# An attention and FFN block on 8 cores: two steps of post work per slot in the first four heads, and two more empty steps after the first LayerNorm

## What is computed

```python
q, k, v = split(x @ Wq + bq), split(x @ Wk + bk), split(x @ Wv + bv)
pattern = einsum('bhid,bhjd->bhij', k, q) * scale      # keys i, queries j
prob = softmax(pattern, axis=-2)                       # over the keys
out = einsum('bhis,bhid->bhsd', prob, v)
x = layernorm(x + concat(out) @ Wo + bo)
h = gelu(x @ w1 + b1)                                  # 1024 -> 4096
x = layernorm(x + h @ w2 + b2)                         # 4096 -> 1024
# x: (8, 4096, 1024) float32
```

## Time and profile before

| | us |
|---|---|
| three runs, median (lowest, highest) | 4659.8 (4652.1, 4875.7) |
| the profiled execution | 4654.3 |
| its span, slowest core (all cores 4628.1 to 4652.4) | 4652.4 |
| TensorE busy | 3593.5 (77%) |
| ScalarE busy | 2305.2 (50%) |
| VectorE busy | 1492.0 (32%) |
| one exp (L812), mean, 2048 of them | 1.023 |

### The profile page before, as it was taken

One profiled execution on the slowest core, in us unless ns is written; L12 is line 12 of the kernel. 1 busy time (PEld: TensorE's weight loads), 2 busy tenths in 40 slices (PEclk: granted clock), 3 DMA queues, 4 the chain that ended last, 5 costly groups with the idle time before them and its releaser, 6 DMA issues.

```text
span 4652.4 us, 57786 instructions; the slowest of 8 cores (4628.1 to 4652.4 us)
## 1 busy us (share of the span) xinstructions
PE 3593.5 (77%) x19264; PEld 1205.1 (26%) x19264; DVE 1492.0 (32%) x1942; ACT 2305.2 (50%) x2191; POOL 193.7 (4%) x344
## 2 busy tenths in 40 slices
PE   4365697887897798778877888788878887888766
PEld 2122242222232232222222222222222222222222
DVE  1133341114223422342234323332333232424243
ACT  0000004884557555765566556655665556555610
POOL 0011100000000000000000000000000000000000
PEclk9677798998999899999998999999999999999977
DMA  8866512113432233133412341234222322332143
GB/s 169 178 158 145 146 64 96 55 55 93 107 78 78 84 94 100 69 93 82 111 60 84 93 113 65 84 88 107 76 84 80 91 82 92 88 84 82 57 89 77
DMA packets 746247, 433.76 MB, mean 93 GB/s; under 512 B 679269, under 2 KB 695781, under 8 KB 728553
## 3 DMA queue, kind: packets, MB, share of 16 engines
q1 hardware_dynamic: 706714, 237.12, 20.7%
q0 software_dynamic: 39248, 192.96, 14.0%
HBM read 377.59 MB, written 77.59 MB: 98 GB/s over the span
## 4 chain that ended last, share of the span: by engine, by line
PE 57%; ACT 14%; DVE 11%; DMA 10%; issue 6%; POOL 1%; SPq 1%; DVEq 0%; ACTq 0%; POOLq 0%
ACT es_sb L812 11%; PE ps_o L822 11%; PE ps_s L799 9%; PE ps_d L834 6%; PE ps_w L668 5%; PE ps_g L712 5%; PE ps_w L712 5%; PE ps_g L668 4%; PE psq L422 2%; ACT h_sb L686 2%; PE psq L318 2%; PE psv L345 2%; DMA xt_f<-xtf_b 2%; DMA wcast<-w 2%; DVE r_sb L865 2%
## 5 line engine op out<-in xcount | busy, mean ns | idle before, releaser
L812 ACT ACTIVATE es_sb<-ps_s 128x1024 bf16<-128x1024 f32 x2048 | 2095.4, 1023 | 1485.5 <-PE ps_s L799 1338.0
L822 PE MATMUL ps_o<-es_sb,v_sb 128*64 128x512 bf16 x4096 | 858.0, 409 | 374.5 <-ACT es_sb L812 314.2
L799 PE MATMUL ps_s<-q_sb,k_sb 64*128 64x512 bf16 x4096 | 817.4, 401 | 108.0 <-DMA q_sb<-q_scr 87.7
L834 PE MATMUL ps_d<-es_sb,ones 128*64 128x512 bf16 x4096 | 839.3, 393 | 0.0
L822 PEld LDWEIGHTS ps_o<-es_sb,v_sb 128*64 128x64 bf16 x4096 | 258.2, 108 | 1019.0 <-issue 1016.1
L799 PEld LDWEIGHTS ps_s<-q_sb,k_sb 64*128 64x128 bf16 x4096 | 193.0, 93 | 972.7 <-issue 972.7
L712 PE MATMUL ps_w<-h_sb,w_sb 128*128 128x512 bf16 x1024 | 258.5, 403 | 77.3 <-ACT h_sb L686 77.3
L863 DVE COPY dD_sb<-ps_d 128x512 f32<-128x512 f32 x64 | 44.3, 691 | 847.1 <-PE ps_d L834 844.9
L668 PE MATMUL ps_w<-h1b_sb,w_sb 128*128 128x512 bf16 x1024 | 265.9, 407 | 59.4 <-DVE h1b_sb L602 52.2
L278 ACT COPY xtf_b<-pst 128x512 f32<-128x512 f32 x64 | 37.5, 586 | 480.2 <-PE pst L270 281.0
L834 PEld LDWEIGHTS ps_d<-es_sb,ones 128*64 128x64 bf16 x4096 | 258.7, 111 | 2.9
(11 more groups left out here) (94 smaller groups left out, 2376.3 us busy)
## 6 DMA issues: line engine op xcount, KB each, us to landing
k_sb<-k_scr POOLq DMA_DIRECT2D x64, 1024.0 KB, 5.4
v_sb<-v_scr POOLq DMA_DIRECT2D x64, 1024.0 KB, 7.7
w_sb<-w_scr SPq DMA_DIRECT2D x256, 256.0 KB, 3.0
w_sb<-w_scr SPq DMA_DIRECT2D x128, 512.0 KB, 4.3
xnat<-x SPq DMA_DIRECT2D x8, 2048.0 KB, 11.5
xt_f<-xtf_b SPq DMA_DIRECT2D x64, 256.0 KB, 2.4
w_scr<-wcast SPq DMA_DIRECT2D x64, 256.0 KB, 3.7
wo_sb<-wo_scr SPq DMA_DIRECT2D x64, 256.0 KB, 3.9
```

Of the source, the lines that this page charges most:

```text
L799: fn = lambda e, p=p, b=b, kc=kc, hh=hh: e.matmul(ps_s[kc % 2][:, hh * 512:(hh + 1) * 512], k_sb[b][hh * 64:(hh + 1) * 64, kc * 128:(kc + ...
L812: "act", lambda e, kc=kc, esb=esb: e.activation(es_sb[esb][:], ps_s[kc % 2][:], AF.Exp, scale=SCALE))
L822: tr.op("pe", lambda e, b=b, kc=kc, esb=esb, hh=hh: e.matmul(ps_o[hh * 64:(hh + 1) * 64, :], v_sb[b][:, kc * 128 + hh * 64: kc * 128 + (hh ...
L834: fn = lambda e, kc=kc, esb=esb, hh=hh: e.matmul(ps_d[hh * 64:(hh + 1) * 64, :], ones64[:], es_sb[esb][:, hh * 512:(hh + 1) * 512], start= ...
```

## The change

Two yields more after the first LayerNorm's tail, so that four empty steps stand there in place of two; and `pump(2)` in place of `pump(1)` after each odd key chunk in the heads 0 to 3. Heads 4 to 7, the extra `pump(2)` at `kc == 3` and the `pump(1)` at a head's end stay.

```diff
@@ make_post, after the first LayerNorm
             yield from emit_ln_tail(y1_sb, h1f_sb, h1b_sb, st1)
+            yield
+            yield
             yield
             yield
             v_ln1 = ln_app
@@ the loop over key chunks
                     if kc + 1 < NKC:
                         do_exp(kc + 1)
                     if kc % 2 == 1:
-                        pump(1)
+                        pump(2 if p < 4 else 1)
                     if kc == 3:
                         pump(2)
```

## The result

The changed kernel takes 4904.4 us in the median, 5.3% more than the kernel before: the ratio is 1.053, with a 95% interval of 1.0515 to 1.0543. On the 4659.8 us of the runs shown ahead that is 4906 us, a microsecond above the upper end of the range given, and 1.1% above the forecast of 4850. In some executions the cores of one die or of both ran at a lower granted clock and took longer: the ratios leave these out and the medians beside them do not, of `dense_rest` a single execution is left, and the profile of `dense_ffn` is of such an execution.

What follows compares the result with a forecast made beforehand. ScalarE was taken to bound attention-only heads (2.27 us a pair), TensorE heads fed FFN matmuls (1.85). Terms summed to +28.0 us a block, +196 us over seven blocks: 4850 us, 4.2% slower, range 4775 to 4905.

Steps and rivals of the forecast that it cites:

- FFN cover: FFN steps beside 28 pairs of key chunks, before 54; 26 pairs return from 1.85 to 2.27 us: +10.9 us a block.
- output projection: Wo steps, paced by VectorE's eviction and statistics, stand beside 4 pairs, before 7: +5.6 us a block.
- LayerNorm chains, both: From sums to broadcast in both LayerNorms, beside 2 pairs, before 4: +1.7 us each, +3.4 a block.
- first apply: After the first LayerNorm, all eight chunks issued in head 0, so FFN1 waits less: -2.5 us a block.
- gelus: First gelu has one FFN step fewer behind it, +1.7; second no longer at a head's end, -3.0: together -1.3 us.
- heads' ends: Ends of heads 0 and 1: two FFN steps wait behind VectorE's norm where one did: +2.0 us a block.
- second apply and outputs: All eight chunks stand ahead of head 2's norm on VectorE, then four outputs every 5.13 us: +9.9 us a block.
- the 4774 us of the most contended engine: Opposing rule: TensorE judged the bound everywhere, a pair always 1.85 us, first term 0; 17.1 us a block, 4774 us.
- The wait for `oO_sb`: Head 3's first value product waits 6 to 7 us, with the second apply ahead of it on VectorE.
- A: Rival: only the cover is lost, added waits overlap; 7 x 11 to 13 us, 4731 to 4745 us; 6 in 100.
- B: Rival: warmer TensorE clock and shorter waits, not slower; -5.5 us a block, 4616 us; 4 in 100.
- C: Rival: FFN1 weight loads can't keep up, up to 0.5 us a step, 16 us a block more, 4960; 10 in 100.

Runs made afterwards that it cites:

- dense_rest: Changed kernel with single steps in the FFN and two per slot elsewhere, in every head; 4819.5 us in one execution, 1.034, no interval.
- dense_ffn: Kernel before with two steps per slot in the FFN steps alone, no yields added; ratio 1.050, median 4905.6 us.
- ffn_aligned: Kernel before with two steps per slot in the FFN and 30 empty steps behind FFN2, holding later stretches at their old slots; 1.029, 4806.9 us.
- after_outy1: Changed kernel with the four outputs staged in quarters of `y1_sb`, so no transpose waits for a store; ratio 1.034, median 4828.0 us.
- chain1_spread: Changed kernel with two empty steps behind the first LayerNorm's sums and two behind its Ln and Exp; ratio 1.055, median 4921.1 us.
- late_apply: Changed kernel with eight empty steps ahead of the second apply, so VectorE does head 2's norm first; ratio 1.058, median 4942.5 us.
- yields_only: Kernel before with the two added yields alone, four empty steps behind the first LayerNorm; ratio 0.998, median 4678.2 us.
- thin: Kernel before without the extra `pump(2)` at key chunk 3 and without the `pump(1)` at a head's end; ratio 1.002, median 4682.5 us.

## Why the prediction was right in direction and short in size

The mechanism held: the filler that ran beside attention was concentrated, four heads lost their cover, and the VectorE and ScalarE chains stand beside fewer pairs. The sum was +28.0 us a block and the traces show +35.9 in block 4. The bounds of its terms, at half their spread, run from 19.4 to 36.4 us a block and so up to 4909 us; the range it stated, from 18 us and up to 4905, was cut a little short at the top. Measured as the prediction defined its terms (elapsed time minus 2.27 us a pair and 1.25 a head's end, block 4 of both traces):

| term | forecast | measured |
|---|---|---|
| FFN cover | +10.9 | +10.9 |
| output projection | +5.6 | +6.5 |
| LayerNorm chains, both | +3.4 | +7.3 |
| first apply | -2.5 | -4.3 |
| gelus | -1.3 | -0.8 |
| heads' ends | +2.0 | +3.9 |
| second apply and outputs | +9.9 | +13.0 |
| sum | +28.0 | +36.5 |

The cover is not measured by itself: it is the 26 pairs at the price that both traces confirm. The last term is 12.1 to the end of the fourth output's transposes (2916.64 - 2877.84 = 38.8 us beside 6 pairs and a head's end), and 0.9 in the slow key chunks behind them. The rows are read one by one and add up to 0.6 more than the block grew.

**Right.** The cover: pitch 5.31 us for 5.3, TensorE full, heads 4 to 7 at 37.6 us each, ScalarE's pace in them unchanged. `ffn_aligned` gives the whole FFN part +16 us a block in its own stretch with the rest in its place, cover, gelus and heads' ends together, where the terms had 10.9 - 1.3 + 2.0 = 11.6; a pair at TensorE's price everywhere (the 4774 us of the most contended engine) is excluded by it and by the windows. The wait for `oO_sb`: 5.83 us for 6 to 7. The projection: the waits of TensorE add up to 1.49 + 1.22 + 0.73 + 1.04 + 3.39 = 7.9 us for "some 8", though the first three, 3.44 us, are for the weights `wo_sb` and not for VectorE, as I had it. Head 3: 56.8 us for "near 55". Of the rivals, A is out (the second apply is a wait) and B went the other way. C, which had 16 us a block, is out at its size but not altogether: in six of the seven blocks one FFN1 step, right behind the norm of head 0, waits 1.31 to 2.50 us for its weights. In block 3:

```profile
2181.88 3.45 PE L670 MATMUL ps_g<-h1b_sb,w_sb 128*128 128x512 bf16 x8 [2.09 <-DMA w_sb<-w_scr]
```

In block 4, from which the table is read, that step waits for VectorE. Before the change such waits are there in one block of the seven beyond 0.3 us.

**The step that failed: the LayerNorm chains, +1.7 each, measured +3.8 and +3.5.** The working took 8.2 us from the sums' end to the broadcast's start beside two pairs. The trace has 2644.69 - 2636.14 = 8.55 us, so the chain itself was nearly right, 0.35 short. Its end was not: the term stopped at the broadcast's start, as if that cost the same before and after. It took 1.98 us before (2546.84 to 2548.82) and 3.78 now (2644.69 to 2648.47), since behind the wait of 3.87 us TensorE ran at 1.2 GHz (the value product right behind it takes 0.64 us in place of 0.41). That is 1.8 us a chain, 3.6 of the 3.9 missed, and it puts the two chains just above the bounds of 0 to 7 that the prediction gave them. I had priced waits at their length, and nothing behind them; the clock stood only in rival B, as something to be won, from the one cold step of the earlier trace rows.

The same price is in two other terms. The sums, for which the last wait of the projection is 3.39 us, take 3.6 us (2632.57 to 2636.14) in place of 1.9, 1.7 more than I took; the term as a whole was short by 0.9. The first FFN step behind a norm takes 3.38 us in place of 1.89, behind a wait of 2.65, and with it the heads' ends come to 3.9 and not 2.0. TensorE, changed kernel, block 4:

```profile
2667.55 1.89 PE L670 MATMUL ps_w<-h1b_sb,w_sb 128*128 128x512 bf16 x8 [2.02 <-DVE h1b_sb L602]
...
2694.40 3.38 PE L670 MATMUL ps_g<-h1b_sb,w_sb 128*128 128x512 bf16 x8 [2.65 <-DVE o_sb L872]
```

The first of these rows is the opposite case: FFN1's first step, whose wait fell from 4.82 to 2.02 us, is no longer cold (1.89 for 3.57), 1.7 us more than I had counted, and that is why the first apply gave 4.3 and not 2.5. This error ran the other way and hid part of the shortfall. In all TensorE is busy 70 us longer on the page, 10 us in each of seven blocks. Not all of it shows in the time, since some of the slow matmuls stand beside another wait.

**Outputs, +13.0 for +9.9.** The order of events and the first wait were right. The four outputs come every 5.7 to 6.3 us and not every 5.13 as in the earlier trace rows, from which I took the period; it belongs to transposes at full clock. The kernel before has a slow round as well, the third, which the earlier trace rows leave out:

```profile
2867.48 1.08 PE L741 MATMUL ps_w<-id_f,h1f_sb 128*128 128x128 f32 x4 [2.32 <-DMA y<-out_sb]
```

From there to the fourth at 2873.10 are 5.62 us, 0.5 more than a round at full clock. In the changed kernel three rounds take 2914.70 - 2896.87 = 17.8 us where 3 x 5.13 are 15.4, 2.4 of the 3.1 missed. Some 1.5 of it is the clock, at 0.5 a round; 0.6 is in the first round, whose copies stand behind the norm's last multiplication on VectorE (2898.00, the copy at 2898.79), and the rest is a store that took longer. `after_outy1` shows what the waits for the stores and the slow transposes cost together: without them the total falls by 89 us (10.6 a block by the medians of the cores, 501.2 for 511.8, and 12 in the last post, which has the same edit).

**What is shown, and what isn't.** Shown by single edits: the store waits (11 us a block), the FFN part with its gelus and heads' ends (16 in its own stretch, 18.5 in the block), the place of LayerNorm and outputs at equal FFN (14, by the intervals 7 to 20). Shown in its place but not in the total: the cold broadcast (`chain1_spread` took away 4.1 us there, and later places took it back). That those places are the cause in `chain1_spread` and `late_apply` is read from their traces; no run held them fixed. `dense_rest` rests on one execution, and the parts measured alone add up to 6 us a block more than the change. Why `dense_ffn` alone costs as much as the change is explained through `ffn_aligned` by its size only, since its own profile gives no block times to compare. The slow matmuls behind waits are read from traces throughout; no run changed the clock and left the waits.

## What to carry to other kernels

A step of TensorE work interleaved with a loop that ScalarE bounds is worth only what it hides, 0.42 us a pair here, but the loop beside it is what hides the chains of VectorE and ScalarE: before bunching steps, count the pairs beside each chain and beside each head's end. Price a wait with what comes behind it at the lower clock, not by its length alone. And an edit that inserts or removes slots moves every later step: four of the twelve experiments with a result (`yields_only`, `thin`, `chain1_spread`, `late_apply`) removed the wait that they were meant to remove and gained nothing, so compare with the later steps held in place, or plan where each lands.

## What was not expected of the hardware

The size of the clock's price in float32 matmuls with one row or one column of output or input: 1.98 us for the four of a broadcast at full clock and 3.78 behind a wait of 3.87 us, while behind a wait of 1.61 us (`chain1_spread`, and the kernel before) they ran at full speed. The wait ahead does not settle it alone: FFN1 steps took 1.89 us behind a wait of 2.02 and 3.38 behind one of 2.65, and on core 4 of the changed kernel one took 1.89 behind a wait of 3.07. Nor does the fall always come at once: behind a wait of 3.20 us in `chain1_spread` the first product of the sums took 1.02 us and the second 1.75. And in the kernel before, the wait of 1.61 us was followed by some 3 us at the lower level as well (value products of 0.64 us at 2543.92 and 2545.45), which were over when the broadcast began. What TensorE did before those waits differed too; no run here separates it. The granted clock fell to 0.57 over 24 us of outputs in which TensorE was busy 14.29 us:

```profile
2632.00:2649.00 17.00, 12.11 (x36) 2.77 (x36) 5.02 (x9) 5.35 (x6) 0.00 (x0) 0.72 0.00 0
...
2893.00:2917.00 24.00, 14.29 (x60) 7.64 (x60) 10.40 (x12) 4.09 (x4) 0.00 (x0) 0.57 0.24 97
```

The two windows of the changed kernel (columns as above) hold the chain and the outputs. The nearest stretches of the kernel before:

```profile
2533.00:2549.00 16.00, 12.69 (x60) 3.22 (x60) 4.94 (x9) 9.95 (x11) 0.00 (x0) 0.89 0.01 1
...
2857.00:2875.00 18.00, 11.88 (x76) 5.89 (x78) 5.15 (x8) 6.66 (x7) 0.00 (x0) 0.91 0.22 88
```

What the columns PEclk show is the fall from 0.89 and 0.91, with short waits, to 0.72 and 0.57, with long ones.
